# The six weight matmuls of a gated unit, from plain fp32 to a high part and a low part of each operand

## The reference

```python
a_tilde = adj + I;  d = rsqrt(sum(adj, axis=1) + 1e-6)
x = layernorm(x + (d[:, None] * a_tilde * d[None, :]) @ (x @ W0))

agg = adj @ x
msg = relu(agg @ W_msg.T + b_msg)
i_r, i_z, i_n = split(msg @ W_ih.T + b_ih)      # W_ih is 384 x 128
h_r, h_z, h_n = split(x @ W_hh.T + b_hh)        # W_hh is 384 x 128
r = sigmoid(i_r + h_r);  z = sigmoid(i_z + h_z)
n = tanh(i_n + r * h_n)
x = layernorm(x + (1 - z) * n + z * x)
```

## The kernel before

| place | TensorE | ScalarE | VectorE |
|---|---|---|---|
| +1 | `x1t_step`: 8 small matmuls turn the state into `p_x` | | |
| +3 | `msg_step`: message matmul (554), three state matmuls (558 to 560) | | `agg_step` (848/851) |
| +5 | `gates_step`: three message matmuls (565 to 567) | `x1t_step` (672) | |
| +6 | | `msg_step` (676) | |
| +9 | | `rz_step`: two sigmoids (681, 682) | `npre_step` (859, 862) |
| +11 | `rows_step`: 4 transposes (575) | `n_step`: tanh (686) | `new_step` (870, 872, 874) |
| +14 | | | `out_stats` (797, 801) |
| +16 | | | `out_step` (807) |

## Time and profile before

### The profile page before, as it was taken

The page is one execution under the profiler, slowest core; times in us unless marked ns, Lnnn a source line. Parts: engine busy times, 40 slices in busy tenths (PEclk is TensorE's granted clock), DMA queues, the critical chain, the costliest instruction groups (busy, mean ns, idle before and its releaser), DMA issues.

```text
span 1844.0 us, 16697 instructions
## 1 busy us (share of the span) xinstructions
PE 1696.3 (92%) x6400; PEld 1160.4 (63%) x6400; DVE 1444.7 (78%) x1346; ACT 641.9 (35%) x560; POOL 117.0 (6%) x110
## 2 busy tenths in 40 slices
PE   0088799997999999999999999999999999999996
PEld 0043344443444556888888888888777777777774
DVE  7888899999999966766666655665877888878785
ACT  0000000000000003445454444444665666566562
POOL 0000000000000011200000000000001011110101
PEclk9999999999999999999999999999999999999998
DMA  9999999999999962666566565665998888989891
GB/s 390 422 386 422 420 423 420 421 416 422 384 422 421 420 236 85 205 196 202 195 197 201 192 201 191 198 196 188 384 314 303 299 302 309 311 291 319 286 313 51
DMA packets 180927, 551.10 MB, mean 299 GB/s; under 512 B 13424, under 2 KB 13936, under 8 KB 148080
## 3 DMA queue, kind: packets, MB, share of 16 engines
q1 hardware_dynamic: 177280, 541.11, 79.4%
q0 software_dynamic: 2560, 8.39, 1.3%
q10 hardware_dynamic: 1008, 0.53, 0.1%
HBM read 545.79 MB, written 4.19 MB: 298 GB/s over the span
## 4 chain that ended last, share of the span: by engine, by line
PE 76%; DVE 12%; DMA 9%; issue 2%; ACT 1%; POOL 0%; SPq 0%; DVEq 0%; ACTq 0%; POOLq 0%
PE bank L487 17%; PE bank L489 17%; PE bank L488 17%; PE bank L435 15%; DMA ring<-adj_blocks 6%; DVE colsum L763 5%; DVE feat L767 2%; DVE feat L770 2%; DMA pool<-adj_blocks 2%; DMA kept<-adj_blocks 1%; PE bank L420 1%; PE bank L554 1%; PE bank L567 1%; PE bank L565 1%; PE bank L457 1%
## 5 line engine op out<-in xcount | busy, mean ns | idle before, releaser
L788 DVE TENSOR_TENSOR lo<-ring,hi 128x2048 fp32r<-128x2048 f32 x206 | 470.2, 2289 | 288.9 <-ACT f L653 209.3
L642 ACT ACTIVATE hi<-ring 128x2048 fp32r<-128x2048 f32 x206 | 394.9, 1918 | 396.2 <-DMA ring<-adj_blocks 239.1
L487 PE MATMUL bank<-hi,x1s 128*128 128x512 f32 x1024 | 416.6, 407 | 3.1 <-DVE lo L788 1.9
L489 PE MATMUL bank<-hi,x1s 128*128 128x512 f32 x1024 | 399.2, 390 | 0.0
L488 PE MATMUL bank<-lo,x1s 128*128 128x512 f32 x824 | 321.1, 390 | 0.0
L435 PE MATMUL bank<-kept,feat 128*128 128x512 f32 x600 | 267.9, 597 | 11.6 <-DMA kept<-adj_blocks 11.6
L487 PEld LDWEIGHTS bank<-hi,x1s 128*128 128x128 f32 x1024 | 192.4, 188 | 52.7 <-issue 7.2
L489 PEld LDWEIGHTS bank<-hi,x1s 128*128 128x128 f32 x1024 | 192.3, 188 | 41.2
L435 PEld LDWEIGHTS bank<-kept,feat 128*128 128x128 f32 x600 | 113.2, 191 | 155.4 <-issue 137.5
L763 DVE TENSOR_TENSOR colsum<-colsum,kept 128x2048 f32<-128x2048 f32 x81 | 185.6, 2291 | 9.9 <-DMA kept<-adj_blocks 8.2
L435 PE MATMUL bank<-ring,feat 128*128 128x512 f32 x376 | 173.9, 610 | 16.0 <-DMA ring<-adj_blocks 16.0
(11 more groups left out here) (99 smaller groups left out, 1600.2 us busy)
## 6 DMA issues: line engine op xcount, KB each, us to landing
ring<-adj_blocks SPq DMA_DIRECT2D x412, 512.0 KB, 5.2
kept<-adj_blocks SPq DMA_DIRECT2D x126, 1024.0 KB, 12.3
ring<-adj_blocks SPq DMA_DIRECT2D x85, 1024.0 KB, 12.2
more<-adj_blocks SPq DMA_DIRECT2D x100, 512.0 KB, 6.0
pool<-adj_blocks SPq DMA_DIRECT2D x45, 1024.0 KB, 12.2
xt<-x_t SPq DMA_DIRECT2D x8, 512.0 KB, 12.1
xin<-x POOLq DMA_DIRECT2D x16, 256.0 KB, 3.5
out<-y POOLq DMA_DIRECT2D x16, 256.0 KB, 4.2
```

Of the source, the lines that this page charges most:

```text
L487: pe.matmul(acc[:, :], fh, ah, start=start and c == 0, stop=False, skip_group_check=True)
L489: mm = pe.matmul(acc[:, :], fl, ah, start=False, stop=stop and c == KC - 1, skip_group_check=True)
L642: ins = act.activation(hi[:, n % NHI], raw(slot_of2[n]), ACT.Copy)
L788: ins = dve.tensor_tensor(flat(low(n)), flat(raw(slot_of2[n])), flat(hi[:, n % NHI]).bitcast(f32), ALU.subtract)
```

## The change

Each of the six products is computed as the tiles' are: weights W = Wh + Wl, operand x = xh + xl, and Wh xh + Wh xl + Wl xh, three fp32r matmuls into the same bank (`gate`). Five things come with it:

- once, behind tile N2 // 4 = 26 of stage two, ScalarE copies both 128x384 weight matrices to their high parts and VectorE subtracts these in place (`split_weights`);
- per row ScalarE writes the transposed state twice (fp32 and fp32r) and the message twice; the state is no longer double-buffered, so its copy now waits for the previous row's `new_ready` and `h_done`;
- per row VectorE makes two low parts, `x1t_lo` at +5 (before out_stats of the previous row) and `msg_lo` at +7 (before out_step of the previous row);
- TensorE's steps move: message matmul from +3 to +4, state matmuls from +3 to +5 (`h_step`), message gates from +5 to +6. ScalarE's `msg_step` moves from +6 to +7;
- the state matmuls wait for `x1t_split`, the message gates for `msg_split`, both from VectorE.

The new buffers take the place of the second state buffer and of a gap; the buffers behind them keep their addresses. The message matmul itself stays plain fp32.

```diff
@@ buffers
-        x1t = sb("x1t", [128, 2, W])
-        msgt = sb("msgt", [128, W])
+        x1t = sb("x1t", [128, W])
+        x1th = sb("x1th", [128, W], f32r)
+        with ExitStack() as s:
+            msgt = sb("msgt", [128, W], at=s)
+        msgl = sb("msgl", [128, W], f32r)
...
-        sb("gap", [128, 4, W])
+        x1tl = sb("x1tl", [128, W], f32r)
+        msgh = sb("msgh", [128, W], f32r)
+
+        wihh_s = sb("wihh_s", [128, 3 * D], f32r)
+        whhh_s = sb("whhh_s", [128, 3 * D], f32r)
+        sb("gap", [128, 2 * D])
...
@@ tensor engine
-                    pe.wait_ge(msg_ready, g)
+                    pe.wait_ge(msg_ready, 2 * g)
...
                 pe.matmul(p_x[:, :], wmsg_s[:, :], tall[:, :], start=True, stop=True).then_inc(msg_done, 1)
-                h = x1t[:, g % 2, :]
+
+            def gate(acc, wh, wl, q, xh, xl, start, stop):
+                cols = slice(q * D, (q + 1) * D)
+                pe.matmul(acc[:, :], wh[:, cols], xh, start=start, stop=False, skip_group_check=True)
+                pe.matmul(acc[:, :], wh[:, cols], xl, start=False, stop=False, skip_group_check=True)
+                return pe.matmul(acc[:, :], wl[:, cols], xh, start=False, stop=stop, skip_group_check=True)
+
+            def h_step(i):
+                g = gru_no[i]
+                pe.wait_ge(x1t_split, g + 1)
                 if g:
                     pe.wait_ge(npre_ready, g)
-                pe.matmul(p_r[:, :], whh_s[:, 0:D], h, start=True, stop=False)
-                pe.matmul(p_z[:, :], whh_s[:, D:2 * D], h, start=True, stop=False)
-                pe.matmul(p_hn[:, :], whh_s[:, 2 * D:3 * D], h, start=True, stop=True)
+                else:
+                    pe.wait_ge(w_split, 1)
+                gate(p_r, whhh_s, whhl_s, 0, x1th[:, :], x1tl[:, :], True, False)
+                gate(p_z, whhh_s, whhl_s, 1, x1th[:, :], x1tl[:, :], True, False)
+                gate(p_hn, whhh_s, whhl_s, 2, x1th[:, :], x1tl[:, :], True, True).then_inc(h_done, 1)
 
             def gates_step(i):
                 g = gru_no[i]
-                pe.wait_ge(msg_ready, g + 1)
-                pe.matmul(p_r[:, :], wih_s[:, 0:D], msgt[:, :], start=False, stop=True)
-                pe.matmul(p_z[:, :], wih_s[:, D:2 * D], msgt[:, :], start=False, stop=True)
-                pe.matmul(p_in[:, :], wih_s[:, 2 * D:3 * D], msgt[:, :], start=True, stop=True).then_inc(gates_done, 1)
+                pe.wait_ge(msg_split, g + 1)
+                gate(p_r, wihh_s, wihl_s, 0, msgh[:, :], msgl[:, :], False, True)
+                gate(p_z, wihh_s, wihl_s, 1, msgh[:, :], msgl[:, :], False, True)
+                gate(p_in, wihh_s, wihl_s, 2, msgh[:, :], msgl[:, :], True, True).then_inc(gates_done, 1)
...
-                i = gru_row(n, 3)
+                i = gru_row(n, 4)
                 if i is not None:
                     msg_step(i)
                 i = gru_row(n, 5)
+                if i is not None:
+                    h_step(i)
+                i = gru_row(n, 6)
                 if i is not None:
                     gates_step(i)
@@ scalar engine
+            def split_weights():
+                act.wait_ge(weights_in, NW * 16)
+                act.activation(wihh_s[:, :], wih_s[:, :], ACT.Copy)
+                act.activation(whhh_s[:, :], whh_s[:, :], ACT.Copy).then_inc(w_hi_ready, 1)
+
             def x1t_step(i):
                 g = gru_no[i]
                 act.wait_ge(x1t_done, g + 1)
-                if g >= 2:
-                    act.wait_ge(new_ready, g - 1)
-                act.activation(x1t[:, g % 2, :], p_x[:, :], ACT.Copy).then_inc(x1t_ready, 1)
+                if g:
+                    act.wait_ge(new_ready, g)
+                    act.wait_ge(h_done, g)
+                act.activation(x1t[:, :], p_x[:, :], ACT.Copy)
+                act.activation(x1th[:, :], p_x[:, :], ACT.Copy).then_inc(x1t_ready, 1)
 
             def msg_step(i):
-                act.wait_ge(msg_done, gru_no[i] + 1)
+                g = gru_no[i]
+                act.wait_ge(msg_done, g + 1)
+                if g:
+                    act.wait_ge(gates_done, g)
                 act.activation(msgt[:, :], p_x[:, :], ACT.Relu, bias=bmsg_s[:, 0:1]).then_inc(msg_ready, 1)
+                act.activation(msgh[:, :], p_x[:, :], ACT.Relu, bias=bmsg_s[:, 0:1]).then_inc(msg_ready, 1)
...
+                if n == N2 // 4:
+                    split_weights()
                 i = gru_row(n, 5)
                 if i is not None:
                     x1t_step(i)
-                i = gru_row(n, 6)
+                i = gru_row(n, 7)
                 if i is not None:
                     msg_step(i)
@@ vector engine
+            def split_weights():
+                dve.wait_ge(w_hi_ready, 1)
+                dve.tensor_tensor(wihl_s[:, :], wih_s[:, :], wihh_s[:, :].bitcast(f32), ALU.subtract)
+                dve.tensor_tensor(whhl_s[:, :], whh_s[:, :], whhh_s[:, :].bitcast(f32), ALU.subtract).then_inc(w_split, 1)
+
+            def x1t_lo(i):
+                g = gru_no[i]
+                dve.wait_ge(x1t_ready, g + 1)
+                dve.tensor_tensor(x1tl[:, :], x1t[:, :], x1th[:, :].bitcast(f32), ALU.subtract).then_inc(x1t_split, 1)
+
+            def msg_lo(i):
+                g = gru_no[i]
+                dve.wait_ge(msg_ready, 2 * g + 2)
+                dve.tensor_tensor(msgl[:, :], msgt[:, :], msgh[:, :].bitcast(f32), ALU.subtract).then_inc(msg_split, 1)
...
                 i = gru_row(n, 3)
                 if i is not None:
                     agg_step(i)
+                if n == N2 // 4:
+                    split_weights()
+                i = gru_row(n, 5)
+                if i is not None:
+                    x1t_lo(i)
+                i = gru_row(n, 7)
+                if i is not None:
+                    msg_lo(i)
                 i = gru_row(n, 9)
                 if i is not None:
                     npre_step(i)
```

More of the change, by code:

```diff
@@ L290, in gnn_resnorm_kernel @@
         wmsg_s = sb("wmsg_s", [128, D])
-        wih_s = sb("wih_s", [128, 3 * D])
-        whh_s = sb("whh_s", [128, 3 * D])
+        with ExitStack() as s:
+            wih_s = sb("wih_s", [128, 3 * D], at=s)
+        wihl_s = sb("wihl_s", [128, 3 * D], f32r)
+        with ExitStack() as s:
+            whh_s = sb("whh_s", [128, 3 * D], at=s)
+        whhl_s = sb("whhl_s", [128, 3 * D], f32r)
         bmsg_s = sb("bmsg_s", [128, 1])
@@ L348, in gnn_resnorm_kernel @@
             sem("x1_ready"), sem("x1_hi_ready"), sem("x1_whole"), sem("spilled"))
-        agg_ready, x1t_done, x1t_ready = sem("agg_ready"), sem("x1t_done"), sem("x1t_ready")
-        msg_done, msg_ready, gates_done, rz_ready = (
-            sem("msg_done"), sem("msg_ready"), sem("gates_done"), sem("rz_ready"))
+        agg_ready, x1t_done, x1t_ready, x1t_split = (
+            sem("agg_ready"), sem("x1t_done"), sem("x1t_ready"), sem("x1t_split"))
+        w_hi_ready, w_split, h_done = sem("w_hi_ready"), sem("w_split"), sem("h_done")
+        msg_done, msg_ready, msg_split, gates_done, rz_ready = (
+            sem("msg_done"), sem("msg_ready"), sem("msg_split"), sem("gates_done"), sem("rz_ready"))
         nmul_done, npre_ready, n_ready = sem("nmul_done"), sem("npre_ready"), sem("n_ready")
@@ L865, in new_step @@
                 g = gru_no[i]
-                h = x1t[:, g % 2, :]
+                h = x1t[:, :]
                 dve.wait_ge(n_ready, g + 1)
```

## The result

The changed kernel takes 1829.7 us, median of four runs (1829.18 to 1829.99), against 1846.07 us for the kernel before (1844.21 to 1848.05); the ratio is 0.9905, 95% interval 0.9893 to 0.9918. The prediction had 1828.0. The profiled execution has 1829.18 us, its span is 1827.4 us, 16.6 less than before.

What follows compares the result with a forecast made beforehand. TensorE was taken to bound the last stage's rows. Gate matmuls 15.9, stall 1.3 and tail 0.2 sum to 17.4 us off 1845.35, giving 1828.0 us; range 1824.5 to 1836.0.

Steps and rivals of the forecast that it cites:

- The bound: Last stage: TensorE is busy for the whole 50 us window, so what it sheds per 32.08 us row comes off the end.
- The gate matmuls: Six products per row on TensorE, 0.857 to 0.68 us each: 15.9 us over fifteen rows, 13.7 by the slower pitch.
- The quarter by the pass count: Three passes for plain fp32's four on TensorE: a gate matmul falls from 0.857 to 0.643 us, 19 us over fifteen rows.
- rival (d): Gate matmul passes on TensorE take 0.214 us each: 19 + 1.3 + 0.2 gained, 1825 us; chance 0.06.
- The stall: TensorE's waits for VectorE's low part on a row's second tile vanish: 1.9 us possible, 1.3 taken, 0 as low end.
- VectorE: Two added subtractions per row fit, 27.9 of 30.9 us; tile 4's low part is 0.6 early; cost 0, up to 7.5.
- Rival (a): Tile 4 on TensorE waits for VectorE's low part each row, 0.5 us a row: 1835.5 us; chance 0.12.
- Rival (b): GpSimd's rstd, blocked by VectorE subtractions, delays out_step and later tiles; out 1.2 us late reckoned, at 3.9 late 1860 us; chance 0.05.
- (c): Split gate matmuls on TensorE get no cheaper than the plain pair, 0.857 us per product: 1845 us; chance 0.04.
- ScalarE, DMA, weights' split: Two more activations a row, denser loads at about 313 GB/s, and the one-time weight split in stage two: each costs 0.
- Tail: Last row, nothing covers added work: later message activation, gates 0.53 us shorter, first sigmoid -0.2 us, between -0.7 and +0.8.
- The sum: Whole kernel: 15.9 + 1.3 + 0.2 = 17.4 us off the median of 1845.35, giving 1828.0 us.

Runs made afterwards that it cites:

- the chain of three, two and one passes: Changed kernel with three fp32r matmuls per gate product (1829.7 us), without the third (1806.59 us), and with only the high parts' matmul (1786.46 us).
- the run whose added work left the row at 479.49 us for 479.50: Changed kernel with all its moved steps, copies and subtractions, but one plain fp32 matmul of high parts per gate product: 1845.62 us, ratio 0.9991.
- two-pass run: Changed kernel without the third matmul of each gate product (low weights times high operand): 1806.59 us, ratio 0.9779.
- the places alone: Kernel before with only the step positions moved, matmuls plain fp32, nothing added on ScalarE and VectorE: 1844.82 us against 1846.81, ratio 0.9987.
- the padded runs: Changed kernel with one, then three unused 128x512 VectorE subtractions in front of tile 4's low part: 1830.44 us, then 1853.12 us.

## Why the prediction was right

- **The bound.** TensorE is full in the rows, and a row's price is its matmuls. Shown by the chain of three, two and one passes, and by the run whose added work left the row at 479.49 us for 479.50.
- **The gate matmuls**, 15.9 us (13.7 by the slower pitch): measured 14.65. The term was 1.25 too large because I took the pitch of the undisturbed stream, 0.227; the new matmuls stand at 0.232, between it and the 0.235 that the earlier trace rows show behind an fp32 block. That an fp32 block stands in front of them does not explain it, as in the two-pass run one does too and the pitch is 0.227. I had both ends and took the upper one without a reason from the rows.
- **The quarter by the pass count** of the Trainium skill (FP8 and Floating Point Precision, TensorE Precision Notes) gives 0.643 us a product and 19 us, which is rival (d); measured is 0.697, a fall of 0.160 for 0.214. Each of the three matmuls takes 0.018 more than a quarter of the plain product. The prediction's reason, that each brings its own weight load, is not shown by any run.
- **The stall**, 1.3 us of a possible 1.9: measured 2.41 with the places alone, all of it and 0.5 more. The excess lies in the first three row distances (1.10, 0.29 and 0.26 less). In the first, an idle time of 0.62 cost more than itself. TensorE before, in front of and behind the matmul at 1367.17 of the earlier trace rows:

```profile
1366.17 0.39 PE L489 MATMUL bank<-hi,x1s 128*128 128x512 f32 x1
...
1367.52 0.40 PE L488 MATMUL bank<-lo,x1s 128*128 128x512 f32 x1
```

  The two steps are 1.00 and 0.35 us where a pitch is 0.23. The 0.09 of the other rows came out about right by luck: the mean wait of 0.31 had the 1.04 and 0.51 of the first two rows in it, and the other twelve are 0.24 each. By the prediction's subtraction those would have cost 0.01. The term errs by 1.1 against the 1.25 above, so the closeness of their sum, 17.06 for 17.2, is in part luck.
- **VectorE** at 0: right, and the walk held to within 0.15 us at each of its steps. Its margin, walked as 0.6, is 0.73 from end to start and 0.5 by the padded runs. Past it the row grows by the full excess. Rival (a) did not come, but it was half a microsecond away.
- **Rival (b)**: rstd took 2.96 us for 1.03, and out_step waited, though 0.40 rather than 1.2 us (1.0 with the places alone). Nothing came of it at TensorE, and taking the wait away gave nothing.
- **Rivals (c) and (d)**: 0.697 is neither 0.857 nor 0.643.
- **ScalarE, DMA, weights' split** at 0: right in the rows. In stage two nothing moved beyond the spread of the wait at its end.
- **Tail**, -0.2: measured -0.23. The message activation comes 0.49 later behind the mark, as the message matmul waits 0.80 us for the second state copy. The gates block begins only 0.16 later: before, it stood behind the state block, 2.37 us behind the activation, and now it waits for the message's low part, 2.04 behind it. From its start to the first sigmoid it is 2.45 for 2.84.
- **The slices.** I read 9 or 10 tenths or just under in all but four of them; the fourth, the fifth and the tenth show 8, 7 and 7. They lie ahead of the last stage, so nothing hangs on it.
- **The sum** was 17.4 and the spans give 16.6. The rest of the difference is the 0.62 before the first row, which no step of mine had; without it the traces give 17.27. Of the 1.7 us between 1828.0 and 1829.7, 0.7 is the starting point: I subtracted from the median of three runs, 1845.35, and that of the four is 1846.07.

## What to carry to other kernels

Count what an fp32 matmul costs by the distance of starts, not by its passes on paper, and compare it with the split form in the same stream: here 0.857 against 0.697 us, worth having only where TensorE is the bound. When another engine has to make the parts, do not ask how much idle time it has in total but where: walk its queue from the last event that the bound engine gives it to the next that it must meet. Move the consumers until the new parts are early, and look at what the moved work had covered where it stood.

## What the runs showed of the hardware

- VectorE and GpSimd: var took 2.14 us and rstd 2.96 beside VectorE's subtractions, 0.19 and 1.03 alone in the tail. Each had begun while a subtraction of 128x2048 was under way; var ended 0.03 us behind that subtraction, rstd 0.87 behind it. The other way round was not seen. In the tail of the changed kernel the message's low part, with both its inputs in SBUF, begins 0.27 us after rstd, and 0.03 after the end of the relu that it waits for; neither is longer than alone:

```profile
1807.39 1.03 POOL L1031 TENSOR_TENSOR rstd<-var,mhalf 128x4 f32<-128x4 f32 x1
1807.66 0.69 DVE L908 TENSOR_TENSOR msgl<-msgt,msgh 128x512 fp32r<-128x512 f32 x1 [0.64 <-ACT msgh L715]
```

  The Trainium skill (SBUF — State Buffer, SBUF: two separate sides) has the lock exclusive for both, whichever starts first. The trace agrees for a GpSimd instruction that comes second, and not for a VectorE one that does: by the page this subtraction would have begun at 1808.42. Spans on GpSimd are rough; VectorE's start and its 0.69 us do not rest on them.
- Of fp32r matmuls of 128x512 in one unbroken stream, most stretches run at 0.227 us and some at 0.232 to 0.235: behind small transposes, behind a plain fp32 matmul, and in the gate blocks of nine, but not in those of six. Why is not tested. It cost this change some 0.1 us a row: the third pass adds 1.50 us to a row where the second adds 1.36.
